# A preln attention block with a feed-forward layer: the chunks' causal mask moved from TensorE to VectorE, and the softmax sums and stage ends put in another order

## The reference, cut to what matters

```python
x = x + _L0_attn_ref(_layernorm(x, axis=-1), L0_attn_W_qkv, L0_attn_W_out)
x = x + _L0_ffn_ref(_layernorm(x, axis=-1), L0_ffn_W, L0_ffn_b, ...)
# _L0_attn_ref
score = jnp.einsum('bihd,bjhd->bijh', q, k) / D ** 0.5
masked_score = score * mask + 1e+30 * (mask - 1.0)      # causal
wmat = jax.nn.softmax(masked_score, axis=2)
out = jnp.einsum('bijh,bjhd->bihd', wmat, v).reshape(b, l, H * D)
return out @ W_out
# _L0_ffn_ref
lilora_weight = up_aux @ (lora_up @ (lora_down @ down_aux))
base = jnp.einsum('bsi,oi->bso', hidden_states, W) + b
delta = jnp.einsum('bsi,oi->bso', hidden_states, lilora_weight)
return base + ALPHA * delta
```

## Time and profile before

| What | us |
|---|---|
| Median of 3 runs | 1955.83 |
| The profiled execution | 1958.16 |
| Its span in the trace | 1955.9 |
| TensorE busy | 1839.4 |
| VectorE busy | 1247.7 |
| GpSimd busy | 1073.3 |
| ScalarE busy | 806.6 |

### The profile page before, as it was taken

One profiled execution on the slowest core, in us unless ns is written; L12 is line 12 of the kernel. 1 busy time (PEld: TensorE's weight loads), 2 busy tenths in 40 slices (PEclk: granted clock), 3 DMA queues, 4 the chain that ended last, 5 costly groups with the idle time before them and its releaser, 6 DMA issues. The chain is left out here.

```text
span 1955.9 us, 34245 instructions
## 1 busy us (share of the span) xinstructions
PE 1839.4 (94%) x13464; PEld 1130.9 (58%) x13464; DVE 1247.7 (64%) x2024; ACT 806.6 (41%) x982; POOL 1073.3 (55%) x583
## 2 busy tenths in 40 slices
PE   7999998999999999999999999999999999997798
PEld 5877775555555555555555555555555555545697
DVE  5465643767676767667676767676767677632465
ACT  3222123444545454544545454545454545453121
POOL 1001002767586857667676767686867667575111
PEclk9999998999999999999999999999999999998899
DMA  5646445212121221212121212121221211031451
GB/s 204 227 175 227 162 167 173 66 45 66 50 66 56 59 66 45 66 45 78 54 73 37 77 39 72 45 69 47 66 72 45 66 45 50 18 117 47 172 194 54
DMA packets 150782, 171.33 MB, mean 88 GB/s; under 512 B 44618, under 2 KB 91744, under 8 KB 150624
## 3 DMA queue, kind: packets, MB, share of 16 engines
q1 hardware_dynamic: 150624, 169.15, 27.4%
HBM read 97.02 MB, written 71.57 MB: 86 GB/s over the span
## 5 line engine op out<-in xcount | busy, mean ns | idle before, releaser
L990 DVE TENSOR_REDUCE f_part_max<-b_ring 128x1 f32<-128x512 f32 (+3 forms) x1200 | 675.2, 604 | 323.6 <-PE b_ring L819 224.3
L921 ACT ACTIVATE b_probs<-b_scores 128x1024 f32<-128x1024 f32 (+3 forms) x640 | 567.5, 899 | 611.9 <-PE b_scores L791 357.6
L1093 POOL TENSOR_TENSOR b_sum_pool<-b_sum_pool,b_probs 128x1024 f32<-128x1024 f32 x288 | 687.0, 2385 | 61.6 <-ACT b_probs L921 31.3
L791 PE MATMUL b_scores<-f_split 64*128 64x512 f32 (+2 forms) x1920 | 269.6, 383 | 9.1 <-ACT b_probs L921 5.5
L791 PE MATMUL b_scores<-b_split 64*128 64x512 f32 (+2 forms) x1920 | 269.2, 382 | 2.8 <-ACT b_probs L921 2.6
L855 PE MATMUL b_o_acc<-b_probs,f_v_in 128*64 128x512 f32 (+3 forms) x1280 | 270.5, 544 | 0.0
L855 PE MATMUL b_o_acc<-b_probs,b_v_in 128*64 128x512 f32 (+3 forms) x1280 | 269.0, 541 | 0.0
L1093 POOL TENSOR_TENSOR b_sum_pool<-b_probs 128x1024 f32<-128x1024 f32 x48 | 116.0, 2417 | 264.0 <-ACT b_probs L921 264.0
L1023 DVE TENSOR_TENSOR g_sum_dve<-g_sum_dve,b_probs 128x768 f32<-128x768 f32 (+2 forms) x192 | 231.3, 1205 | 30.2 <-ACT b_probs L921 24.4
L791 PEld LDWEIGHTS b_scores<-b_split 64*128 64x128 f32 x1920 | 166.3, 186 | 50.5 <-issue 21.2
L791 PEld LDWEIGHTS b_scores<-f_split 64*128 64x128 f32 x1920 | 168.0, 187 | 45.8 <-issue 21.1
(11 more groups left out here) (135 smaller groups left out, 2250.4 us busy)
## 6 DMA issues: line engine op xcount, KB each, us to landing
f_raw<-k_t SPq DMA_DIRECT2D x32, 512.0 KB, 4.8
f_raw<-q_t SPq DMA_DIRECT2D x32, 512.0 KB, 5.6
g_recip<-r_t SPq DMA_DIRECT2D x128, 128.0 KB, 3.0
o_t<-g_o_norm SPq DMA_DIRECT2D x64, 256.0 KB, 2.0
q_t<-a_stage_a SPq DMA_DIRECT2D x32, 256.0 KB, 2.3
q_t<-a_stage_d SPq DMA_DIRECT2D x32, 256.0 KB, 2.1
k_t<-a_stage_a SPq DMA_DIRECT2D x32, 256.0 KB, 2.0
k_t<-a_stage_d SPq DMA_DIRECT2D x32, 256.0 KB, 2.0
```

The costliest lines, as they stand in the source:

```text
L791: last = nc.tensor.matmul(scores[s % 2][:, h, lo:TILE], lhs, b[u][head(h), queries], start=(term == 0), stop=(term == 3 and not diagonal))
L921: nc.scalar.activation(probs[s % PR][:, :, off:], scores[s % 2][:, :, off:], ACT.Exp, scale=scale).then_inc(exp_done, 1)
L990: nc.vector.tensor_reduce(part_max[:, h, ib, c:c + 1], rowwise[h][:, 0:width], AX.X, ALU.max).then_inc(chunk_reduced, 1)
L1093: nc.gpsimd.tensor_tensor(sum_pool[:], first, probs[s % PR][:], ALU.add).then_inc(pool_added, 1)
```

## The change

The items below are the edits, numbered for the text.

1. The four mask products of a diagonal chunk (L827) go. VectorE adds a mask `causal`, made once by GpSimd, and takes the maximum in one call (`tensor_tensor_reduce`), with the chunk in the accumulator memory as one input, `causal` in SBUF as the other, and the sum written over the chunk.
2. The denominators are four products with 32 columns of ones, each over 256 of the 512 queries of one head, instead of two with 64 columns over 512. They fill 4 x 32 partitions of one bank's first 256 columns. `den_row` has half the columns, ScalarE copies half as many, and the row is spread with four transfers of half the size instead of two.
3. GpSimd's first add of a tile waits until VectorE has done its last add (d = 3) of the tile before; it waited for the first (d = 0).
4. In the last item VectorE adds the blocks j = 8 to 11 of the last tile too, and takes `sum_pool` in after d = 1. GpSimd is left with j = 1 to 7 there. The last item's `normalise` is queued at unit 6 instead of 10.
5. The wait for the first part's stores moves behind the barrier, to the start of attention's SyncE queue.
6. In the output stage the load of the third tile goes ahead of `finish_last_o`, and the small weight loads (L1241) go behind a wait for the first tile's low part.

The diff, cut to its core:

```diff
@@ attention: who adds what @@
+    LATE_FULL = 4
+    def dve_adds(n, s):
+        t, j = units[s]
+        return j >= NB * t or (n == LAST_ITEM and t == TI - 1 and j >= NB * t - LATE_FULL)
...
@@ invert (finish_last_o alike) @@
-                    for h in range(2):
-                        sp.dma_start(den_spread[:, h, :], den_row[h * D:h * D + 1, :].rearrange(
+                    for c in range(4):
+                        h, half = divmod(c, 2)
+                        sp.dma_start(den_spread[half * D:(half + 1) * D, h, :], den_row[c * P // 4:c * P // 4 + 1, :].rearrange(
...
@@ chunk_products @@
-                                                start=True, stop=not diagonal)
-                    if diagonal:
-                        for side in range(2):
-                            cols = slice(width - P + side * D, width - P + (side + 1) * D)
-                            for h in range(2):
-
-                                last = nc.tensor.matmul(rowwise[h][:, cols], early_queries(h, side),
-                                                        consts["pick"][head(h), :], start=False, stop=(side == 1))
+                                                start=True, stop=True)
...
@@ denominators @@
-                    for h in range(2):
-                        last = nc.tensor.matmul(denom[head(h), :], consts["ones"][:, 0:D],
-                                                sum_dve[t % 2][:, h, :], start=True, stop=True)
+                    for c in range(4):
+                        h, half = divmod(c, 2)
+                        cols = slice(half * DEN, (half + 1) * DEN)
+                        last = nc.tensor.matmul(denom[c * P // 4:(c + 1) * P // 4, 0:DEN], consts["ones"][:, 0:P // 4],
+                                                sum_dve[t % 2][:, h, cols], start=True, stop=True)
...
@@ reduce_chunk @@
                     for h in range(2):
-                        nc.vector.tensor_reduce(part_max[:, h, ib, c:c + 1], rowwise[h][:, 0:width], AX.X,
-                                                ALU.max).then_inc(chunk_reduced, 1)
+                        if c == ib // NB:
+                            nc.vector.tensor_tensor_reduce(rowwise[h][:, 0:width], rowwise[h][:, 0:width],
+                                                           causal[:, TILE - width:], 1.0, LOWEST, ALU.add, ALU.max,
+                                                           part_max[:, h, ib, c:c + 1]).then_inc(chunk_reduced, 1)
+                        else:
+                            nc.vector.tensor_reduce(part_max[:, h, ib, c:c + 1], rowwise[h][:, 0:width], AX.X,
+                                                    ALU.max).then_inc(chunk_reduced, 1)
...
@@ GpSimd's item @@
-                                pool.wait_ge(dve_added, n * DIAG + NB * (t - 1) + 1 + NB)
+                                pool.wait_ge(dve_added, sum_ready[n, t - 1])
...
-                        for late in late_tile(n, s - 10, previous):
+                        for late in late_tile(n, s - (10 if following else 6), previous):
                             normalise(*late)
...
@@ SyncE, start of attention @@
                 sp.sem_inc(o_stored, 1)
+                for of_engine in lead["stored"]:
+                    for of_stage in of_engine:
+                        sp.wait_ge(of_stage, lead["all_stored"])
...
@@ SyncE, output stage @@
                 load_x(0, 0)
+
+                wait_apart(sp, o_lo_ready, PARTS, first_loaded[0], 16)
...
+                load_o(2, 0, slice(0, KC), o_loaded[0])
+                step(0, 0, True, False, False)
                 finish_last_o()
-
-                wait_apart(sp, o_lo_ready, PARTS, first_loaded[0], 16)
-                load_o(2, 0, slice(0, KC), o_loaded[0])
-                step(0, 0, True, True, False)
+                wait_apart(sp, x1_ready, 1 + 2, first_loaded[0], 16)
+                load_x(2, 0)
```

More of the change, by code:

```diff
@@ L189, in project_qkv @@
         emptied = [sem("emptied_a"), sem("emptied_d")]
-        stored = [[sem(f"stored_{e}{i}") for i in range(STAGES)] for e in "ad"]
+        stored = lead["stored"]
         def sink(T, g):
@@ L257, in _ @@
                     tile(T, T % 2, T + 2 < tiles)
-                for e in range(2):
-                    for s in range(STAGES):
-                        sp.wait_ge(stored[e][s], 16 * (tiles * HALF // STAGES) + 1)
+                lead["all_stored"] = 16 * (tiles * HALF // STAGES) + 1
             @block.tensor
@@ L614, in attention, with first_dve @@
     ring_last = ring_order(False)[1]
-    POOL_ADDS = sum(NB * t - 1 for t in range(1, TI))
+    LATE_FULL = 4
+    def dve_adds(n, s):
+        t, j = units[s]
+        return j >= NB * t or (n == LAST_ITEM and t == TI - 1 and j >= NB * t - LATE_FULL)
+    def first_dve(n, t):
+        return next(j for j in range(NB * (t + 1)) if dve_adds(n, starts_of[t] + j))
+    starts_of = {t: s for s, t in starts.items()}
+    freed, pool_done, dve_before, sum_pool_read, sum_ready = {}, {}, {}, {}, {}
+    pool_adds = dve_ops = 0
+    for n in range(2 * PAIRS):
+        for s, (t, j) in enumerate(units):
+            if dve_adds(n, s):
+                dve_before[n, s] = dve_ops
+                dve_ops += 1
+                freed[n, s] = ("dve", dve_ops)
+                full = first_dve(n, t) < NB * t
+                if full and j == NB * t + 1:
+                    dve_ops += 1
+                if t and (j == NB * t + 1 if full else j == NB * t):
+                    sum_pool_read[n, t] = dve_ops
+                sum_ready[n, t] = dve_ops
+            elif j:
+                pool_adds += 1
+                freed[n, s] = ("pool", pool_adds)
+                if j == 1:
+                    freed[n, s - 1] = ("pool", pool_adds)
+                pool_done[n, t] = pool_adds
     AHEAD = 2
     PR = 8
-    POOL_AHEAD = PR - NB
     LOS = 2 * TI
@@ L913, in exponentials @@
                     act.wait_ge(pv_done, n * U + s + 1)
-                    tp, jp = units[s - PR]
-                    back = 1 if s < PR else 0
-                    if jp >= NB * tp:
-                        act.wait_ge(dve_added, n * DIAG + jp + 1 + NB - back * DIAG)
-                    else:
-                        adds = sum(NB * q - 1 for q in range(1, tp)) + max(jp, 1)
-                        act.wait_ge(pool_added, n * POOL_ADDS + adds + POOL_AHEAD - back * POOL_ADDS)
+                    if (n, s) >= (0, PR):
+                        adder, count = freed[(n, s - PR) if s >= PR else (n - 1, s - PR + U)]
+                        act.wait_ge(dve_added if adder == "dve" else pool_added, count)
                     nc.scalar.activation(probs[s % PR][:, :, off:], scores[s % 2][:, :, off:], ACT.Exp,
@@ L1007, in add_unit @@
                     d = j - NB * t
[L1008 removed]
+                    off = max(d, 0) * P
                     dve.wait_ge(exp_done, n * U + s + 1 + 2)
[L1011 removed]
+                    if j == first_dve(n, t) and (t == 0 or d < 0):
                         nc.vector.tensor_copy(sum_dve[t % 2][:], probs[s % PR][:]).then_inc(dve_added, 1)
                         return
[L1014 to L1017 removed]
+                    if j == first_dve(n, t):
+                        dve.wait_ge(pool_added, pool_done[n, t])
                         nc.vector.tensor_tensor(sum_dve[t % 2][:], sum_pool[:], probs[s % PR][:],
@@ L1221, in finish_last_o @@
                     sp.wait_ge(tail["den_copied"], o_tiles + 1)
-                    for h in range(2):
-                        sp.dma_start(tail["den_spread"][:, h, :], tail["den_row"][h * P // 2:h * P // 2 + 1, :].rearrange(
-                            "o (p i) -> o p i", i=NB)).then_inc(tail["den_moved"], 16)
+                    for c in range(4):
+                        h, half = divmod(c, 2)
+                        sp.dma_start(tail["den_spread"][half * P // 2:(half + 1) * P // 2, h, :],
+                                     tail["den_row"][c * P // 4:c * P // 4 + 1, :].rearrange("o (p i) -> o p i", i=NB)
+                                     ).then_inc(tail["den_moved"], 16)
                     sp.wait_ge(tail["inverted"], o_tiles)
@@ L1307, in _ @@
                 out_project(0, 0, [0, 1, 2, 3])
-                pe.wait_ge(tail["dve_added"], DIAG_UNITS * 2 * all_pairs + NB)
-                for h in range(2):
-                    half = slice(h * P // 2, (h + 1) * P // 2)
-                    last = nc.tensor.matmul(last_denom[half, :], consts["ones"][:, 0:P // 2],
-                                            tail["sum_dve"][last_t % 2][:, h, :], start=True, stop=True)
+                pe.wait_ge(tail["dve_added"], tail["dve_ops"])
+                for c in range(4):
+                    h, half = divmod(c, 2)
+                    cols = slice(half * DEN, (half + 1) * DEN)
+                    last = nc.tensor.matmul(last_denom[c * P // 4:(c + 1) * P // 4, :], consts["ones"][:, 0:P // 4],
```

(2 more changed lines are left out.)

51 lines of the change are left out of this document (27 added, 24 removed).

## The result

The changed kernel takes 1933.86 us, the median of 4 runs (1931.07 to 1937.32), against 1956.69 for the kernel before on the same chip: a ratio of 0.9883 (95% interval 0.9865 to 0.9901), 22.8 us less. The forecast was 56 less.

The account below looks back on a forecast made before the run. TensorE, busy 1293.8 of 1352 us in attention, was taken as the bound. Items -34 and tail -22 gave -56 from the profiled 1958.16, so 1902.2; the median lies 2.3 below: 1900 us, range 1848 to 1936.

Parts of the forecast that it names:

- the likeliest one: The forecast itself: items save 34 us, the tail 22, together 56; 1900 us, own range 1880 to 1914, chance 0.44.
- GpSimd held, at the item's start: Start of each item: late spread and reciprocal delay TensorE's next chunk; net -0.3 us per item, -5 over 15 items.
- Denominators: Denominator products: four side by side cost 0.53 us instead of 0.86, saving 0.33; 48 outside the first stretch give -16.
- Masks: Diagonal chunks: TensorE saves 0.05 us per mask, 12 in all; VectorE's pass costs what it replaces, its readout 0.13.
- the wait near unit 21: TensorE's small wait within an item grows by the slower diagonal reductions: +0.4 x 15 = +6 us.
- The d = 3 adds and the large waits: VectorE's d = 3 adds fall from 2.3 to 0.42 us; TensorE's three large waits per item go, the third giving -11.
- The border: After the last item: TensorE's idle 9.08 us shrinks by 7.8, and the lower clock after it gives -2.5.
- The last item: Last item: `normalise` of tile 0 moves ahead of tile 2's sums, whose denominators are 3 to 4 us late: +4.
- Output stage and start: Output stage: earlier third-tile load gives -13.8 us, lower clock after it -1.7; start of attention: 0 (ends -2 and 0).
- The third rival: Waits after diagonal chunks take back all attention saves; only the tail's 22 us left: 1934 (1925 to 1955), chance 0.10.
- The first rival: Everything comes through, with GpSimd's delay shorter or the reciprocal not holding TensorE: 1861 us (1840 to 1880), chance 0.20.
- The fourth: Rival: VectorE's masked reductions are held up by GpSimd's adds; slower, 1968 to 2145 us, middle 2050, chance 0.11.

Follow-up runs that it names:

- e2: Changed kernel with SyncE issuing the four spreading transfers of tile 0 ahead of the store of the item before's last tile: 1854.6 us, ratio 0.9481.
- e8: Kernel before with edit 2 alone (four denominator products, four transfers): 1942.5 us, ratio 0.9930.
- e10: e2 with edit 1 undone (masks back on TensorE, plain reductions on VectorE): 1862.3 us, ratio 0.9518.
- e11: e2 with edit 3 undone (GpSimd's first add of a tile waits for VectorE's first diagonal add only): 1911.9 us, ratio 0.9776.
- e6: Changed kernel with the last item's normalisation queued at unit 10 again: 1932.4 us, ratio 0.9875.
- e3: Changed kernel with the denominators spread by two transfers of two rows each instead of four of one row: 1896.2 us, ratio 0.9703.
- e1: Changed kernel with VectorE's reciprocals two units later in its queue (unit 7 after a tile's start instead of 5): 1906.8 us, ratio 0.9741.

## Why the prediction was wrong

The time lies in the range, but it got there by another way than the likeliest one: 22.8 us instead of 56. Step by step:

**GpSimd held, at the item's start (failed).** The prediction had this chain: the spread late by the hold and by two more issues, the reciprocal behind them, the next chunk behind that, "net -0.3 per item". Measured from the first denominators of item 6 (880.06 before, 873.13 after), the reciprocal was forecast at +22.2 to +22.8 and came at +22.3, and the chunk at +22.7 and came at +23.1. So the lateness was right to 0.4 us, in part by luck. The sum had 0.9 us for the hold and nothing for the normalisation that meets VectorE's add, which adds 1.0 (2.26 instead of 1.28); it had up to 2.1 us from the last issue to the reciprocal, where 1.2 were enough. What failed is what follows from the lateness: units 0 to 12 were to save 0.3 us on balance, and they lose 2.3. I had booked the waits that go and the one that comes as if only their sum counted. But three short waits became one of 3.3 to 4.3 us, and behind it the clock fell, a cost that the sum put at nothing although I had charged that same effect at the border. The clock costs 2.3 us per item in the mean (e2's windows against these), 14 x 2.3 = 32 us, about the whole shortfall of 33. The other misses nearly cancel: the later chunk (6 us) and the border (6) against 8 more than forecast in units 12 to 40 and 3 in item 0. Item 8, with the same wait of 3.35 us and no fall, has 20.7 us instead of 23.3.

**Denominators (right).** The step in is 902.75 to 904.62, 1.87 instead of 1.77, the step out 0.57 instead of 0.96: 0.29 saved, forecast 0.33, and the 0.10 of the new shape is there. If only two ran side by side, the step out would have stayed at 0.96, so the four do. The drain rule of the Trainium skill ("TensorEngine Tiling (Array Packing)", Key Properties), which spoke against the change, agrees with the 0.10; the 0.39 saved on the way out outweighs it. e8, with this edit alone, is 14.2 faster.

**Masks (right in sum, by two terms that are both too small).** The masked pass of 512 takes 0.716, the readout 0.14, forecast 0.61 to 0.69 and 0.13. In e10 the net worth is 7.8 us, where the forecast's own terms give 12 for all masks less 6 for the wait near unit 21. By the estimate above it is 21.5 less 13.7, so both terms were about half of what they are.

**The d = 3 adds and the large waits (right).** 0.418 in the mean, and the waits behind them are gone; units 12 to 24 and 24 to 40 save 2.50 per item, forecast 1.93. In e11 edit 3 is worth 57 us, 53 of them waits (72.5 less 19.2), as much as the earlier trace rows had.

**The border (mis-sized).** Forecast -10.3, measured -4.6: TensorE is still idle 4.51 us and then at the lower clock (0.69 in the first window). VectorE's full adds take 5.46 us for two beside GpSimd's instead of 2.4, so the last ones are late:

```profile
1765.88 5.46 DVE L1052 TENSOR_TENSOR g_sum_dve<-g_sum_dve,b_probs 128x1024 f32<-128x1024 f32 x2
```

```profile
1776.00:1786.00 10.00, 5.49 (x32) 5.13 (x29) 5.59 (x6) 4.19 (x2) 0.00 (x0) 0.69 0.30 84
1786.00:1796.00 10.00, 10.00 (x86) 9.48 (x84) 3.23 (x1) 0.01 (x1) 0.00 (x0) 0.97 1.00 372
```

**The last item (right in sum, by luck).** The wait for tile 2's denominators is 5.56 us, forecast 3 to 4, and units 24 to the last lose 8.0. Units 0 to 24 save 3.7, which the forecast did not have. In them a wait for tile 1's denominators has gone, which before was:

```profile
1733.18 1.08 PE L865 MATMUL b_ring<-g_sum_dve,p_ones 128*64 128x512 f32 x4 [2.42 <-DVE g_sum_dve L1023]
```

The item as a whole is at +4.3, forecast +4.

**Output stage and start (right).** -15.5 forecast and -14.2 measured for the former; 0 forecast and -1.5 for the latter, inside its bounds. No run shows that edit 5 makes these 1.5: the first product with v comes at 323.4 to 325.2 us in the runs with the edit (325.20 in e6) and at 324.1 to 325.2 in those without.

The third rival had the size and its kind of cause: waits behind diagonal chunks take back what attention saves. It had no mechanism for it. The first rival (1861) is what the same edits give with the queue mended (1854.6). The fourth is refuted: in 472 masked passes the longest is 734 ns, though GpSimd is busy for 73% of the time, and no pass of any width is over 70 ns longer than the shortest of that width (512 columns: 698 to 734); the rule of the Trainium skill ("SBUF — State Buffer", SBUF: two separate sides), that VectorE with a pair of inputs of which one is not in SBUF is not locked out by GpSimd, agrees with it.

The experiments show that the clock's fall goes with the wait: in e2, without the wait, it falls in none of the 14 windows. Why it did not fall in item 8, in nine items of e3 and in six of e1 is open. The waits are no shorter there: 3.35 us in item 8 and 3.33 in item 6; in e3 2.25 in the first window shown and 2.29 in the second; in e1 3.02 us in item 11, without a fall, and 2.14 in item 6, with one.

## What to carry to other kernels

Before a faster bound engine is counted as gain, follow each chain with its own pace (transfers, a store ahead of them in a queue) from the same starting point, and ask by how much the engine now arrives before it. A hold that ends one meeting of VectorE and GpSimd can bring about another: here it took 1.4 us off VectorE's d = 3 add and put 1.0 on the normalisation. Where several short waits melt into one long one, price the clock as well: here 2.3 of 5.7 us. A transfer that a strict queue waits for should not be issued behind a store that waits for a third engine: moving it ahead was worth 79 us in the changed kernel and 2 in the one before.

## What the runs showed of the hardware

The masked pass with one input in accumulator memory and one in SBUF took at most 734 ns in 472 passes (716 in the mean at 512 columns) beside a GpSimd that is busy 73% of the time. GpSimd's multiply (1.28 us alone) took 2.26 and VectorE's add of two SBUF tiles 1.63 instead of 1.22 where they met. One transfer of two separate rows is issued in the time of one of a single row (1.17 us for two against 2.40 for four).
